# A GNN layer on one core: ladder bases by TensorE, sorting work of VectorE respread, last row one-hots shared

## The reference

```
h = relu(layernorm(x))
e = silu(concat(h[src], h[dst], w) @ eW1 + eb1)
e = silu(e @ eW2 + eb2)
agg = segment_sum(e, src)
out = x + silu(concat(h, agg) @ nW1 + nb1) @ nW2 + nb2
```

## Time and profile before

| what | value |
|---|---|
| runs (3) | 3905.82 us median, 3905.34 to 3907.06 |
| profiled execution | 3906.85 us |
| its span, first to last instruction | 3904.7 us |
| busy over the span | PE 2884.9 (74%), DVE 2246.1 (58%), ACT 1831.7 (47%), POOL 2377.9 (61%) |
| mean granted TensorE clock | 0.893 |
| rows of the sorting stage, first L1198 to last L988 | 83.1 to 881.4 us |
| first instruction of the edge stage on PE (L1065) | 905.4 us |

### The profile page before, as it was taken

The page is one execution under the profiler, slowest core; times in us unless marked ns, Lnnn a source line. Parts: engine busy times, 40 slices in busy tenths (PEclk is TensorE's granted clock), DMA queues, the critical chain, the costliest instruction groups (busy, mean ns, idle before and its releaser), DMA issues.

```text
span 3904.7 us, 84571 instructions
## 1 busy us (share of the span) xinstructions
PE 2884.9 (74%) x23063; PEld 2460.8 (63%) x23064; DVE 2246.1 (58%) x7954; ACT 1831.7 (47%) x4225; POOL 2377.9 (61%) x2353
## 2 busy tenths in 40 slices
PE   7999999994667666666677676666666666766668
PEld 4777777773666556656566666666665666666567
DVE  8999999974444444444444444444444444444445
ACT  3999999992333333333333333333333333333332
POOL 1788888885555555555555555555555555555550
PEclk8999999997888888888888888888889888888889
DMA  2111111111222222222222222222222222221113
GB/s 73 27 24 24 28 24 24 28 25 36 45 44 44 45 45 43 45 45 43 45 45 44 44 45 45 44 45 44 45 45 44 44 45 45 44 45 41 41 41 137
DMA packets 371974, 168.98 MB, mean 43 GB/s; under 512 B 295766, under 2 KB 341390, under 8 KB 371854
## 3 DMA queue, kind: packets, MB, share of 16 engines
q0 software_dynamic: 72992, 121.26, 12.4%
q1 hardware_dynamic: 276670, 35.71, 6.0%
q10 hardware_dynamic: 22192, 10.53, 0.9%
HBM read 138.64 MB, written 28.67 MB: 43 GB/s over the span
## 4 chain that ended last, share of the span: by engine, by line
another core or an unknown queue 40%; PE 29%; ACT 15%; DVE 7%; issue 6%; ACTq 2%; DMA 0%; POOL 0%; DVEq 0%; SPq 0%; POOLq 0%
PE bk L1087 10%; ACT ED L1267 6%; PE bk L988 4%; PE bk L1085 4%; ACT BIG L1198 3%; PE bk L1077 3%; ACT BIG L1206 2%; ACT ED L1272 1%; DVE GA L636 1%; ACT ED L1262 1%; ACTq L1275 1%; PE bk L1075 1%; PE bk L910 1%; PE bk L1154 1%
## 5 line engine op out<-in xcount | busy, mean ns | idle before, releaser
L485 POOL DMA_INDIRECT GA<-q_d,IX x1760 | 1702.0, 967 | 1216.5 <-remote 717.7
L833 DVE TENSOR_TENSOR BIG<-bk,BIG 128x128 f32 x1760 | 513.6, 292 | 1533.1 <-remote 703.7
L1267 ACT ACTIVATE ED<-bk,eb1c 128x512 f32<-128x512 f32 x440 | 302.3, 687 | 1485.3 <-remote 1379.3
L1085 PE MATMUL bk<-B,ones 128*128 128x512 bf16 x440 | 190.4, 433 | 820.5 <-ACT ED L1267 820.0
L1077 PE MATMUL bk<-OHS,P 128*128 128x128 bf16 x5280 | 655.0, 249 | 0.0
L1075 PE MATMUL bk<-identf,GA 128*128 128x128 f32 x1760 | 577.6, 328 | 60.7 <-issue 46.7
L1085 PEld LDWEIGHTS bk<-B,ones 128*128 128x128 bf16 x440 | 43.1, 98 | 898.8 <-ACT ED L1267 686.5
L1077 PEld LDWEIGHTS bk<-OHS,P 128*128 x5280 | 544.0, 115 | 54.9
L1087 PEld LDWEIGHTS bk<-W,ED 128*128 128x128 f32 x3520 | 562.2, 228 | 17.7
L1087 PE MATMUL bk<-W,ED 128*128 128x128 f32 x3520 | 564.2, 313 | 0.0
L1096 PE MATMUL bk<-ED 128*128 128x128 f32 x3520 | 535.3, 298 | 32.2 <-ACT ED L1272 22.1
(11 more groups left out here) (206 smaller groups left out, 3725.1 us busy)
## 6 DMA issues: line engine op xcount, KB each, us to landing
GA<-q_d,IX POOLq DMA_INDIRECT x1760
RB<-rec_d SPq DMA_DIRECT2D x440, 8.0 KB
q_d<-QS SPq DMA_DIRECT2D x14, 448.0 KB
u_d<-QS ACTq DMA_DIRECT2D x98, 64.0 KB
P<-u_d SPq DMA_DIRECT2D x8, 768.0 KB, 10.4
rec_d<-BIG,GA POOLq DMA_INDIRECT x312
rec_d<-ED SPq DMA_DIRECT2D x16, 220.0 KB, 9.9
HT<-hT_d ACTq DMA_DIRECT2D x99, 32.0 KB
```

The source lines that it names most:

```text
L485: e.indirect_dma_start(G[k % 4 * U + u], None, q_d, bass.IndirectOffsetOnAxis(ap=IX[k][:, u:u + 1], axis=0))\
L833: e.tensor_tensor(AGG[:, ds(v, P)], banks[6 + k % 2][:, u * P:(u + 1) * P], AGG[:, ds(v, P)], ALU.add).then_inc(s["ad"], 1)
L1085: e.matmul(z[:, :], ones[:, :], B2[:, :, :].rearrange("p a b -> p (a b)"), start=True, stop=False)
L1267: e.activation(E1[k % 2], banks[2 + k % 2][:, :], ACT.Silu, bias=eb1c[:, :]).then_inc(s["e1"], 1)
```

## The change

1. **Bases.** `base` on ACT and the tile `DG` are gone. At u = 0 PE makes the base by four matmuls: the weights are one column of `lbR` repeated 128 times, the moving operand is the first 99 columns of the fp32 identity, and each writes every fourth of the bank's 396 columns. It waits for `dq` (set once) in place of ACT's `lbb`.
2. **Parts in odd steps.** `norm1` and `norm2` become six parts at t0 + 1, 3, ... 11, with t0 six steps earlier (18 + 30 q); what hangs on them (`root` at +8, `flip` at +12 and +15, `tohT` at +14 and +17, blocks from +18) keeps its absolute step. `places` of both pairs of a round, `records` and `indexed`: `places` always in an odd step (for even pairs one step later), `records` in v % 8 = 3 and `indexed` in 4 (each one step later); `scatter` and `join` one step later; SP's step line starts at 28 instead of 32. There is one more step at the end.
3. **No AFn.** ACT takes |AF - iota| by scale -1, so DVE's negated copy goes.
4. **Last 16 rows** (`LAG` = 8, rows 400 to 415). DVE's new `rowhot` makes the first two of each row's four one-hots, POOL makes none, ACT the last two; PE waits for `a2` there.
5. PE's two extra fillers for each row from step 432 on are gone.

The core of the diff:

```diff
+        LAG = 8
         def lone(v):
-            return v % 2 == 0
+            return v % 2 == 0 and v < NR - 2 * LAG
+        def taken(v):
+            return 2 if v >= NR - 2 * LAG else int(lone(v))
...
-                t0 = 24 + 30 * q
+                t0 = 18 + 30 * q
...
-                            at.setdefault(t0 + 12 + 3 * b + name, []).append((f, q, b))
+                            at.setdefault(t0 + 18 + 3 * b + name, []).append((f, q, b))
...
-                e.tensor_scalar(AFn[k][:, :], i1[:, :], -1.0, None, ALU.mult)
...
+            def rowhot(v):
+                e.wait_ge(s["ps"], v // NU + 1)
+                ge(e, s["so"], v - 3)
+                o = v % NU * GC
+                for k in range(2):
+                    ins = e.tensor_scalar(AO[v % 4][:, k, :], iof[:, :], AF[v // NU % 2][:, o + k:o + k + 1], None,
+                                          ALU.is_equal)
+                ins.then_inc(s["a2"], 1)
...
-            node = node_steps(((0, 0, norm1), (0, 4, norm2), (4, None, rest1), (8, None, rest2)))
+            node = node_steps(((0, 1, mean), (0, 3, centre), (0, 5, squares), (0, 7, variance), (0, 9, scaled), (0, 11, relu),
+                               (4, None, rest1), (8, None, rest2)))
...
-                if t < NSLOT and step(t) and step(t)[1] == NU - 1:
-                    places(step(t)[0])
+                for x in (t - 1, t) if t % 2 else ():
+                    if x < NSLOT and step(x) and step(x)[1] == NU - 1:
+                        places(step(x)[0])
...
-                if v >= 8 and v % 8 == 2:
+                if v >= 8 and v % 8 == 3:
                     records(v // 8 - 1)
-                if v >= 8 and v % 8 == 3:
+                if v >= 8 and v % 8 == 4:
                     indexed(v // 8 - 1)
...
+                if NR - 2 * LAG <= v + 1 < NR:
+                    rowhot(v + 1)
...
-                    e.wait_ge(s["lbb"], 4 * i + 4)
-                    e.matmul(z, onesf[:, :], DG[:, :],
-                             start=True, stop=False, skip_group_check=True).then_inc(s["bi"], 1)
+                    e.wait_ge(s["dq"], 1)
+                    for r in range(4):
+                        e.matmul(z.rearrange("p (b r) -> p r b", r=4)[:, r, :],
+                                 lbR[:, 4 * i + r:4 * i + r + 1].broadcast_to([P, P]), identf[:, 0:NBIN],
+                                 start=(r == 0), stop=False, skip_group_check=True)
...
+                elif taken(v):
+                    e.wait_ge(s["a2"], v - (NR - 2 * LAG) + 1)
...
-                    if t >= NSLOT:
-                        warm()
-                        warm()
...
-            def base(i):
-
-                e.wait_ge(s["dq"], 1)
-                ge(e, s["bi"], i)
-                for r in range(4):
-                    e.activation(DG[:, :].rearrange("p (b r) -> p b r", r=4)[:, :, r], identf[:, 0:NBIN], ACT.Copy,
-                                 scale=lbR[:, 4 * i + r:4 * i + r + 1]).then_inc(s["lbb"], 1)
...
-                for k in range(lone(v), GC):
+                for k in range(taken(v), GC):
                     ins = e.activation(AB[v % 2][:, k, :], iof[:, :], ACT.Abs,
-                                       bias=AFn[v // NU % 2][:, o + k:o + k + 1])
+                                       scale=-1.0, bias=AF[v // NU % 2][:, o + k:o + k + 1])
...
-                if t % NU == NU - 6 and t < NR - NU:
-                    base(t // NU + 1)
```

More of the change, by code:

```diff
@@ L171, in gnn @@
         AF = [ga([P, 2 * SC], fp32) for k in range(2)]
-        AFn = [ga([P, 2 * SC], fp32) for k in range(2)]
         BF = [ga([P, 2 * SC], fp32) for k in range(2)]
@@ L356, in _ @@
             load_next(0)
-            for t in range(32, OFF + 8 * (NS + 2)):
-                q = (t - 32) // 30
-                if (t - 32) % 30 == 0 and q <= NCH:
+            for t in range(28, OFF + 8 * (NS + 2)):
+                q = (t - 28) // 30
+                if (t - 28) % 30 == 0 and q <= NCH:
                     if q + 1 < NCH:
@@ L463, in join @@
                                      SIDE[q % 4][0:NB, :], None, compute_op=ALU.add).then_inc(s["acc"], 16)
-            for v in range(-1, 8 * (NS + 2) + 4):
+            for v in range(-1, 8 * (NS + 2) + 5):
                 if v + 1 < NR and lone(v + 1):
@@ L469, in _ @@
                     clear()
-                if v % 8 == 3 and v >= 27:
+                if v % 8 == 4 and v >= 28:
                     join(v // 8 - 3)
-                for q, c in ((v // 8 - 1, v % 8 - 4), (v // 8 - 2, v % 8 + 4)):
+                for q, c in ((v // 8 - 1, v % 8 - 5), (v // 8 - 2, v % 8 + 3)):
                     if 0 <= q < NS and 0 <= c < CHB:
@@ L722, in bc, with mean @@
                 return t.rearrange("p (b f) -> p b f", f=1).broadcast_to([P, CB, NF])
-            def norm1(q, _):
+            def mean(q, _):
                 X = XC[q % 2]
@@ L734, in norm1, with squares, variance, scaled @@
                     e.memset(X[:, CB - 1, :], 0.0).then_inc(s["ms"], 1)
+            def squares(q, _):
                 link(e.tensor_tensor(SQ[:, :, :], XM[:, :, :], XM[:, :, :], ALU.mult))
+            def variance(q, _):
                 link(e.tensor_reduce(st[:, 2, :], SQ[:, :, :], axis=AX.X, op=ALU.add))
                 e.tensor_scalar(st[:, 2, :], st[:, 2, :], 1.0 / NF, EPS, ALU.mult, ALU.add).then_inc(s["var"], 1)
-            def norm2(q, _):
+            def scaled(q, _):
                 e.wait_ge(s["rt"], q + 1)
@@ L758, in rest2 @@
                                 P3[1][:, o:o + HF], ALU.subtract).then_inc(s["p3"], 1)
-            node = node_steps(((0, 0, norm1), (0, 4, norm2), (4, None, rest1), (8, None, rest2)))
+            node = node_steps(((0, 1, mean), (0, 3, centre), (0, 5, squares), (0, 7, variance), (0, 9, scaled), (0, 11, relu),
+                               (4, None, rest1), (8, None, rest2)))
             link_m, marks = {}, {}
             e.wait_ge(s["zero"], 16 * 16)
-            for t in range(NR + OFF + 4):
+            for t in range(NR + OFF + 5):
                 v = t - OFF
@@ L1025, in pq @@
                          W1ab[:, :, :].rearrange("p a b -> p (a b)"), start=True, stop=True).then_inc(s["pq"], 1)
-            node = node_steps(((0, 6, lambda q, _: flip(q, 0)), (0, 9, lambda q, _: flip(q, 1)), (0, None, pq)))
-            for t in range(NR + OFF + 4):
+            node = node_steps(((0, 12, lambda q, _: flip(q, 0)), (0, 15, lambda q, _: flip(q, 1)), (0, None, pq)))
+            for t in range(NR + OFF + 5):
                 v = t - OFF
@@ L1242, in _ @@
             cnt(NF1 - 1)
-            base(0)
             e.wait_ge(s["edc"], 48)
             e.activation(VAL[:, :, 1:2], TWv.rearrange("p (c w) -> p c w", w=1), ACT.Copy).then_inc(s["vw"], 1)
-            for t in range(NR + OFF + 4):
+            for t in range(NR + OFF + 5):
                 v = t - OFF
-                if t % NU == NU - 6 and t < NR - NU:
-                    base(t // NU + 1)
                 if 0 <= v < NR:
```

12 lines of the change are left out of this document (7 added, 5 removed).

## The result

The change runs in 3914.74 us, the median of 14 runs (3908.58 to 3929.89); the kernel before, beside it on the same chip, in 3905.76 us (3903.07 to 3908.01, 14 runs). The ratio is 1.003, with a 95% interval of 1.0019 to 1.004: slower by 9 us, where 3881 was forecast. The profiled execution took 3929.89 us, the longest of the 14, with a span of 3928.1; it shows all causes at once. Its span is 23.4 us over that of before where the medians differ by 9, so its stretches are longer than those of most runs.

A forecast was written before the change was run, and what follows sets the result against it. ACT was taken to bound the sorting stage, DVE close behind. Gains of 21 us in the body and 4.5 in the last rows, less 0.4 at the start, made 25.1 us: 3881 us forecast, range 3873 to 3896.

The forecast's parts named there:

- So ACT sets the pace: Body, rows 0 to 400: ACT, idle only 26 of 765 us, was taken as the bound, with DVE close behind.
- The term of 24.6 us: Body: moving 23 bases off ACT, 1.07 us each, takes 24.6 us off the engine said to set the pace.
- The root keeps its step, and the variance now ends in the step just before: Norm: ACT's square root stops waiting for DVE's variance, saving at most 9.0 us.
- What it can give is waiting: Norm parts in odd steps: no work removed, but waits of DVE 28.8, PE 22.0 and ACT 9.0 us could shrink.
- The floors: Body: least time each engine alone would need, ACT 731.4, PE 730.5 and DVE 733.4 us.
- Bases on PE: Body: four strided matmuls take 0.9 us a base, 0.14 more than now, 3.2 us in all on PE.
- third rival: Body: the strided PSUM write is slow and PE becomes the bound, 3925 us at four times the cost; chance 0.08.
- Last 16 rows: End of the sorting stage: 31 us falls to 26.5, a gain of 4.5 us, with PE's clock left full.
- what the sorting stage gains moves the edge stage forward unchanged: Sorting to edge stage: any gain carries over in full, provided the last rows gain it too.
- The first: Rival, body: DVE takes over and the spread gives nothing, 3899 us, a gain under 10; chance 0.17.
- the root's wait under 3 us: Sign in the profile after: ACT's idle time before the norm's square root falls under 3 us.
- Edge stage: Stage after sorting: said to keep its length to about 1 us.

The follow-up runs named there:

- e4: The kernel before with only the bases moved from ACT to PE; 3945.13 us against 3946.5 for the kernel before, ratio 0.9997.
- e7: The change run again unaltered, on chip C; 3202.54 us against 3189.85 for the kernel before, ratio 1.0043.
- e5: The change with norm parts re-spaced: variance three steps ahead of root, relu three ahead of flip; 3176.7 us against 3189.85 for the kernel before, ratio 0.9961.
- e10: e5 with the bases made by ACT again; 3181.14 us against 3191.32 for the kernel before, ratio 0.9972.
- e6: The change with the norm in one piece, LAG = 0 and PE's fillers back; 3187.99 us against 3189.85 for the kernel before, ratio 0.9994.
- e9: e5 with the norm's relu moved from DVE to ACT; 3196.65 us against 3191.32 for the kernel before, ratio 1.0015.
- e1: The change with the norm's first four parts, mean to variance, four steps earlier; 3952.03 us against 3946.5 for the kernel before, ratio 1.0016.
- e8: The kernel before run again unaltered, on chip C; 3190.29 us against 3189.85 beside it.
- e2: The change with the norm in one piece again, at the steps of before; 3935.76 us against 3946.5 for the kernel before, ratio 0.9971.
- e11: e5 without DVE's share of the last 16 rows (LAG = 0, fillers back); 3179.13 us against 3191.32 for the kernel before, ratio 0.9961.
- e3: The change with PE's two extra fillers per row from step 432 put back; 3959.5 us against 3946.5 for the kernel before, ratio 1.0031.

## Why the prediction was wrong, point by point

**"So ACT sets the pace": the step that failed.** It was read from the idle column: ACT idle least, and only at the root. But an engine with little idle time can be held there by others, and ACT's one wait, the root's, was the place. e4 took 22 us of work from ACT and the body did not move (766.0, 766.6). The term of 24.6 us was right as work and nothing as time. The body as a whole, forecast 21 us shorter, came out 16.5 us longer in the profile of the result and 9.6 in e7. Once the norm is spread with room it is worth 3.7 us (e5 against e10). So the two parts don't add: the norm holds the pace first, and ACT comes next, 10 us below it.

**"The root keeps its step, and the variance now ends in the step just before": true, and the cause of the loss.** I took the steps for a clock that all engines share, and an end one step earlier for early enough. The engines share no clock; ACT runs ahead of DVE by as much as its buffers and PE's `place` let it. From the waits I estimate between two and three steps of 1.9 us at this point: it waits 3.1 us (40.0 over 13) for a part that stands one step ahead, about 2 us for one two steps ahead (25.3 over 13 in e6, 27.0 over 13 in e9), and not at all for one three steps (e5) or five (e1) ahead. Before, the room was two steps too, and it waited 0.7 us; without the bases it gets further ahead, and waits 2.4 (31.1 over 13 in e4). So the bases' leaving and the narrower room worked against each other, and I had counted both as gains. The term was -9.0 us of waiting and came out as +34. The diff had the same for `flip`, which I didn't look at: `relu` was two steps ahead of it and is now one. Of what the two cost, e1 shows 11 us for the root; the pair of `relu` and `flip` has no run of its own, and e1 against e5 (17 us) is across two chips.

**"What it can give is waiting".** That is right of the spread as such, with room: e5's body is 13.2 us shorter than before (e8), 9.4 of them by the spread (e6 against e5), and DVE's idle time is 18 us in place of 28.8 (I had chosen 10.6). In the change as it stands the spread made waits: DVE's went to 48.

**The floors were about right:** DVE works 734.9 us (733.4 said), ACT 717.3, with its own pauses of 18.3 us 735.6 (731.4 said). PE's 740.1 is over my 730.5, in part because its granted clock dropped: over 4 us windows from 86 to 846 us, it fell under 0.9 in seven places in the change, in four before, in none in e5, where PE works 724.1 us. The start of the rows, 0.4 us later by the sum, came 1.1 us later (1.0 in e7).

**Bases on PE:** 0.86 to 0.97 us (0.9 said). By the Trainium skill's rule ("Advanced Engine Details and Errata", PSUM Cachelines), which the prediction weighed as its third rival, it should have been clearly above what four such matmuls take into neighbouring columns, and that is 0.86 to 0.97 us as well. The trace disagrees with the rule for fp32 matmuls of this width, and the rival falls. **AFn and `places`:** the body falls by 3.8 us in e6 against e8, which has the bases on PE too; 2.8 were reckoned for AFn.

**Last 16 rows:** 24.6 to 24.9 us at full clock in e2, e5 and e7, for 26.5 said; up to the last matmul the term was right in size. Not reckoned: the clock at 0.52 in the profiled execution. I had named it and left it, on the ground that PE would stay nine tenths busy; that holds for the mean (37.1 of 40.0 us), and what came before the drop was one wait of 2.78 us. And not reckoned: POOL, to which I gave "room" by its share in the body. In the last rows the records of the last two slices come 7.0 us apart (855.21 and 862.23 us in e5), and a slice costs POOL 9.4; so some 2.6 of the 5.5 us are lost before the first gather, and on C and D the rest by the last one (e11). So the premise that what the sorting stage gains moves the edge stage forward unchanged did not hold for this term.

**The rivals.** The first said that DVE takes over and the spread gives nothing: right on the bases, but it too took the spread for harmless. None had a new wait as its mechanism, though the root's idle row and the diff's two numbers (variance at 7, root at 8) held all it needed. What was listed as a sign, the root's wait under 3 us, was the sign that failed. The signs "PE's waits for `ranks` under 10 us" would not have held in the good version either: 23.5 us in e5. **Edge stage:** said to keep its length within 1 us; it moved by -5.5 us here and by +3.6 on C, with the same code. On C and D the shift goes with the share of the last rows (e11); what does it, and what does the -5.5 us on A, stays open.

**The sum, on one chip** (e7 against e8): start +1.0, body +9.6, last rows -5.7, way to the first gather +3.6, gathers +3.6: 12.1 us, the difference of the two spans (3200.2 - 3188.1).

On A and B the first gather of the kernel before (or of e4) comes 21 us behind the last row, on C 19. The traces show where the 2 us stand: DVE's copy of the last slice (L684) starts at 883.53 us on A, 2.1 us behind the last matmul's end (881.43), and on C 0.1 us behind it:

```profile
881.90 0.21 DVE L684 CAST GA<-bk 128x48 int32<-128x48 f32 x1 [5.57 <-PE bk L988]
```

From that copy to the first gather both take 19 us (19.1, 18.9). With the share the copy starts 2.8 to 5.9 us behind on A and B (the change, e1, e2, e3), and the gather comes 18.6 to 19.0 us behind the copy; on C and D it is 0.1 and 22.5 to 22.8 us. So POOL is the limit there on C and D only. Why the copy starts late on A and B stays open.

## What to carry to other kernels

Where several engines walk one numbered line of steps, count the room of a producer against how far its consumer runs ahead, not against the step number: here one step cost 3 us of waiting for each norm, and three steps none. To find what sets the pace, don't take the engine that is idle least, look at the one short wait that it does have; here it was on an engine which was itself in a burst, and taking work from the first gave nothing (e4). And an engine's idle sum is no allowance for a new wait on it: 36 us of idle time did not cover 13 waits of 2 us (e9); PE stood for ACT's one-hots ten times, 11.2 us in all.

## What the runs showed of the hardware

- A matmul's write to every fourth fp32 column of a PSUM bank cost no more than to neighbouring ones: four of 99 columns in 0.86 to 0.97 us, four of 96 in 0.86 to 0.97 (0.87 in the earlier trace rows).
- One wait of PE of 2.78 us was followed by 32 us at a granted clock of 0.52, with PE busy for 29.9 of them; in e1 one of 2.40 us by 13.4 us at 0.50. In e2, e5 and e7 the same rows ran at 1.00, and there no wait of PE in them was over 0.84 us. In the body of e8 the clock fell four times, for some 3.5 us each, beside waits of 1.8 to 2.3 us.
- POOL issues one indirect DMA of this kind each 1.26 us, a join each 1.87; a slice of 8 rows needs 6 x 1.26 + 1.87 = 9.4 us of it.
- The kernel before took 3905.8 us on chip A, 3946.5 on B, 3190 on C and 3191 on D; between A and C, where both were profiled, the first to last gather makes 708 us of the 717 that the spans differ by.
